# A decoder of six layers on one core: experts' weights prepared inside the experts' loop, and a rewritten quantised feed-forward

## The reference

```python
x = x + L0_attn(layernorm(x))     # 16 heads of 64, output projection, + x, layer norm, gamma, beta
x = x + L0_xattn(layernorm(x))    # attention over ctx (8, 64, 256), weights rounded to 256 levels
x = x + L0_ffn(layernorm(x))      # 8 groups: 256 -> 1024 -> 256, own weights for each group
x = x + L1_attn(layernorm(x))     # 8 experts, 2 for each row
x = x + L1_xattn(layernorm(x))    # masked attention over ctx, 16 heads of 16
x = x + L1_ffn(layernorm(x))      # quantised pair
```

## Time and profile before

| | us |
|---|---|
| median of 3 runs (2390.36 to 2404.99) | 2395.47 |
| the profiled execution | 2393.87 |
| its span, first to last instruction | 2392.2 |
| PE, DVE, ACT, POOL busy | 1696.3, 1606.5, 1374.0, 817.9 |
| PE's mean granted clock (1.00 is 2.4 GHz) | 0.855 |

### The profile page before, as it was taken

How to read it: one execution, slowest core, us unless ns; L and a number is a source line. 1 busy time by engine, 2 the same in 40 slices (tenths; PEclk the granted TensorE clock), 3 DMA queues, 4 the chain that set the end, 5 groups by cost and what they waited for, 6 DMA issues and landing times. The chain is left out here.

```text
span 2392.2 us, 43530 instructions
## 1 busy us (share of the span) xinstructions
PE 1696.3 (71%) x13405; PEld 1078.5 (45%) x13405; DVE 1606.5 (67%) x3129; ACT 1374.0 (57%) x2171; POOL 817.9 (34%) x751
## 2 busy tenths in 40 slices
PE   4889898989899898985899802223454677774855
PEld 1455555555555555553677601211222355553323
DVE  6867777787878778775233386735773767675774
ACT  3788888888878798881454412433553323333543
POOL 0434545454445454451000050570001444451042
PEclk9999999999999999996798955556666888987778
DMA  6222222222222222222122111422112111111002
GB/s 179 61 50 61 60 53 63 61 50 63 61 50 63 57 60 56 61 48 96 36 71 72 36 75 53 151 78 88 53 35 71 38 33 23 30 26 47 0 1 71
DMA packets 173941, 139.90 MB, mean 58 GB/s; under 512 B 83808, under 2 KB 155539, under 8 KB 173506
## 3 DMA queue, kind: packets, MB, share of 16 engines
q1 hardware_dynamic: 166850, 122.91, 19.8%
q0 software_dynamic: 6912, 14.71, 2.8%
HBM read 62.05 MB, written 20.97 MB: 35 GB/s over the span
## 5 line engine op out<-in xcount | busy, mean ns | idle before, releaser
L588 ACT ACTIVATE a_p_hi<-ps,a_probs_up,a_s_scale 128x512 f16<-128x512 f32 x512 | 397.9, 777 | 79.8 <-ACTq L586 79.2
L589 ACT ACTIVATE a_probs<-ps,a_probs_up,a_s_scale 128x512 f32<-128x512 f32 x512 | 398.4, 778 | 0.0
L690 DVE TENSOR_REDUCE a_top<-ps 128x2 f32<-128x1024 f32 x256 | 312.7, 1221 | 121.5 <-DVEq L689 121.5
L914 POOL TENSOR_TENSOR a_p_lo<-a_probs,a_p_hi 128x1024 f16<-128x1024 f32 x128 | 284.8, 2225 | 179.3 <-POOLq L913 163.9
L902 POOL TENSOR_TENSOR a_ops<-a_ident_down,a_top 64x256 f16<-64x256 f32 x256 | 158.8, 620 | 395.9 <-POOLq L897 387.4
L699 DVE TENSOR_TENSOR a_p_lo<-a_probs,a_p_hi 128x1024 f16<-128x1024 f32 x128 | 184.6, 1443 | 37.2 <-DVEq L698 37.2
L452 PE MATMUL ps<-a_ops 128*128 128x512 f16 x512 | 196.3, 383 | 13.5 <-PEq L450 13.5
L471 PE MATMUL ps<-a_v_hi,a_p_hi 128*128 128x65 f16 x2048 | 203.2, 196 | 2.2 <-PEq L466 2.2
L438 PE MATMUL ps<-a_qk,a_qd 128*128 128x512 f16 x512 | 153.4, 381 | 72.2 <-PEq L436 72.2
L474 PE MATMUL ps<-a_v_lo,a_p_hi 128*128 128x64 f16 x2048 | 203.2, 194 | 0.0
L475 PE MATMUL ps<-a_v_hi,a_p_lo 128*128 128x65 f16 x2048 | 203.0, 195 | 0.0
(11 more groups left out here) (482 smaller groups left out, 3782.2 us busy)
## 6 DMA issues: line engine op xcount, KB each, us to landing
a_ops<-a_qk SPq DMA_DIRECT2D x384, 128.0 KB, 2.4
f_w<-in_L_ffn_W_dram SPq DMA_DIRECT2D x16, 1024.0 KB, 7.4
a_qd<-a_qk SPq DMA_DIRECT2D x128, 64.0 KB, 2.3
g_a<-in_L_attn_gp_w_dram SPq DMA_DIRECT2D x8, 1024.0 KB
X<-in_x_dram SPq DMA_DIRECT2D x8, 512.0 KB, 9.9
expert_in<-g_w SPq DMA_DIRECT2D x8, 512.0 KB
g_a<-in_L_attn_dp_w_dram SPq DMA_DIRECT2D x8, 512.0 KB
e_x_in<-expert_in SPq DMA_DIRECT2D x8, 512.0 KB, 4.3
```

The source lines that it names most:

```text
L588: nc.scalar.activation(p_hi[:, h % 2, k, :], scores, ACT.Exp, bias=probs_up[:], scale=s_scale[:])
L589: nc.scalar.activation(probs[:, h % 2, k, :], scores, ACT.Exp, bias=probs_up[:], scale=s_scale[:]).then_inc(st_taken, 1)
L690: nc.vector.tensor_reduce(top[:, c % 2, 2 * pair:2 * pair + 2], ps[:, ROW:ROW + 2, :], AX.X, ALU.max).then_inc(row_taken, 1)
L914: nc.gpsimd.tensor_tensor(p_lo[:, h % 2, 2:KT, :], probs[:, h % 2, 2:KT, :], p_hi[:, h % 2, 2:KT, :], ALU.subtract).then_inc(p_made_pool, 1)
```

## The change

- **Self-attention.** DVE computes only minus the mean (128x1); ACT subtracts it (`centre`, 128x256, in heads 4, 6, 8, 10, ahead of `heads_out`); POOL multiplies by gamma (`times_gamma`, 128x512, in heads 8 and 12). DVE waits for both (`z_made`) in head 13. The last batch, behind the loop, is unchanged.
- **Middle.** `f_rows` and `f_rows_out` move behind the next scores and the last two groups of `w2T`, on PE and on ACT, and in the table of banks.
- **Experts.** `ExpertWeights` (below) has buffers of its own for two experts' raw weights; `upT` and `downT` hold three experts. Routing prepares experts 0 and 1 and sums the magnitudes of expert 2. In the loop, now written out for all eight experts, expert e's DVE queue rounds expert e+2, PE and ACT turn and copy expert e+1 in three pieces, all through PSUM bank 2, and ACT sums the magnitudes of e+3. The three Newton steps of an expert go from DVE to POOL. SP loads an expert's weights four ahead.
- **Masked attention** loads the pair's weights behind its mask.
- **Quantised pair.** The weights' peaks come before the row moments. The last tile of each sequence is normalised by ACT. The turns of rows and weights are interleaved. b2 is a column (two transposes of small rows), so its work is on 128x2 and not 128x256, and stands behind the semaphores that start the second pass. In the second pass outputs are computed with columns of the result as partitions (L2946's place: 512 columns each), scaled and shifted by ACT (first half) and DVE (second half), turned back by PE (eight f32 transposes a sequence) and added to `X` by DVE. PE takes a quarter of an output half behind each `h` bank. POOL has nothing left to do. The store of a sequence is issued when its rows are done, and `store_block` is gone.

The core of the diff:

```diff
# self_attention, DVE, head loop
-                            centre(t)
+                            nc.vector.tensor_scalar(less_mean[:, t:t + 1], ln_y.mean_var[:, t, 0:1], -1.0, None, ALU.mult)
+                            dve.drain().then_inc(y_means, 1)
# self_attention, ACT and POOL
+                    nc.scalar.activation(z[:, t, :], y[:, t, :], ACT.Identity, bias=less_mean[:, t:t + 1])
...
+                    nc.gpsimd.tensor_tensor(z[:, halves[half], :], z[:, halves[half], :], each(gam), ALU.mult)
# middle, PE (ACT likewise)
-                    if b:
-                        for c in range(DC):
-                            f_rows(b - 1, c)
                     if b + 1 < B:
                         scores(b + 1, bank_of["scores", b + 1])
                     if b < B:
                         turn_w2(b, 2)
                         turn_w2(b, 3)
+                    if b:
+                        for c in range(DC):
+                            f_rows(b - 1, c)
# experts: the new class
+class ExpertWeights:
...
+    def magnitudes(self, act, n):
+        nc, j = self.core.nc, n % 2
+        act.wait_ge(self.loaded[j], 32)
+        act.sem_inc(self.loaded[j], -32)
+        for i, part in self.parts:
+            nc.scalar.activation(self.junk[:, part], self.stage[:, j, part], ACT.Abs, accum_out=self.sums[:, j, i:i + 1])
+        act.drain().then_inc(self.part, 1)
+
+    def total(self, pe, n, bank):
+        nc, j = self.core.nc, n % 2
+        pe.wait_ge(self.part, 1)
+        pe.sem_inc(self.part, -1)
+        pe.wait_ge(self.out, 1)
+        nc.tensor.matmul(self.core.ps[:, bank, 0:2], self.ones[:], self.sums[:, j, :], start=True, stop=True).then_inc(self.total_full, 1)
+
+    def lower(self, dve, n, bank):
+        nc, j = self.core.nc, n % 2
+        dve.wait_ge(self.total_full, 1)
...
+        for i, part in self.parts:
+            nc.vector.tensor_scalar(self.below[:, part], self.stage[:, j, part], self.minus_half[:, j, i:i + 1], None, ALU.is_lt)
+
+    def ternary(self, dve, n):
...
+            nc.vector.scalar_tensor_tensor(out=self.w3[:, part], in0=self.stage[:, j, part], scalar=self.half[:, j, i:i + 1],
+                                           in1=self.below[:, part], op0=ALU.is_gt, op1=ALU.subtract)
+        dve.drain().then_inc(self.round, 1)
+        if n + 2 < self.E:
+            dve.drain().then_inc(self.used, 1)
+
+    def turn(self, pe, n, piece, bank):
...
+        pe.wait_ge(self.out, 1)
+        pe.sem_inc(self.out, -1)
...
+    def turned_out(self, act, n, piece, bank):
...
+        nc.scalar.activation(dst, self.core.ps[:, bank, :].bitcast(BF16), ACT.Copy).then_inc(self.out, 1)
# experts' loop, ACT
+                        weights_out(e + 1, 0)
+                        gate(j, 2)
+                        square_hidden(j, 2)
+                        weights_out(e + 1, 1)
+                        gate(j, 3)
+                        square_hidden(j, 3)
                         act.drain().then_inc(h_squared_all, 1)
                         if not first:
                             results((j + 1) % 2)
+                        weights_out(e + 1, 2)
                         if not last:
                             rows_out()
...
+                        if e + 3 < E:
+                            weights.magnitudes(act, e + 3)
# experts' loop, PE
+                        turn_weights(e + 1, 0)
                         up(e, 2)
+                        turn_weights(e + 1, 1)
                         up(e, 3)
                         if not first:
                             down(e - 1)
+                        turn_weights(e + 1, 2)
+                        if e + 2 < E:
+                            weights.total(pe, e + 2, WEIGHT_BANK)
# experts' loop, DVE
                         hidden(j, 2)
                         hidden(j, 3)
+                        if e + 2 < E:
+                            weights.lower(dve, e + 2, WEIGHT_BANK)
                         hidden_rows(e, j)
# hidden_rows, DVE: seed here, three Newton steps of four operations on POOL
-                        rsqrt(nc, dve, rstd[:], value[:], half[:], tmp[:])
...
+                        dve.drain().then_inc(seeded, 1)
+                        if e + 2 < E:
+                            weights.ternary(dve, e + 2)
+                        dve.wait_ge(rooted, 1)
# quantised_pair, PE, second pass
+                for b in range(B + 1):
                     for c in range(FC):
+                        if b < B:
+                            hidden_again(b, c)
+                        if b >= 2 and c == BACK_AT:
+                            turn_back(b - 2)
+                        if b:
+                            outputs(b - 1, c)
+                turn_back(B - 1)
```

More of the change, by code:

```diff
@@ L622, in batch @@
                             powers(h, k)
+                        if finish and h - 2 in PROJ_B:
+                            centre(PROJ_B[h - 2])
                         if h in TURN and (h > 1 or finish):
@@ L1906, in _ @@
[L1906 to L1917 removed]
+                    pe.sem_inc(weights.out, 1)
@@ L1919, in _ @@
+                    pe.sem_inc(weights.w3_used, 1)
+                    for n in range(2):
+                        weights.total(pe, n, WEIGHT_BANK)
+                        for piece in range(DC + 1):
+                            weights.turn(pe, n, piece, WEIGHT_BANK)
                 @block.vector
@@ L2241, in _ @@
                     gate(0, 1)
-                    expert(0, last=False, first=True)
-                    with act.Fori(0, E // 2 - 2) as pair:
-                        expert(1, last=False)
-                        expert(0, last=False)
-                    expert(1, last=False)
-                    expert(0, last=False)
-                    expert(1, last=True)
+                    for e in range(E):
+                        expert(e)
                     whole(r2[:], h[:, 1], h_round, r2_made)
@@ L2313, in _ @@
                     up(0, 1)
-                    expert(0, last=False, first=True)
-                    with pe.Fori(0, E - 2) as e:
-                        expert(e + 1, last=False)
-                    expert(E - 1, last=True)
+                    for e in range(E):
+                        expert(e)
                     turn_hidden()
@@ new lines, in hidden, with hidden_again @@
+                def hidden(b, c, bank):
+                    for m in range(DC):
+                        last = nc.tensor.matmul(ps[:, bank, :], w1T[:, m, c * P:(c + 1) * P], x8[:, m, b * S:(b + 1) * S],
+                                                start=(m == 0), stop=(m == DC - 1))
+                    return last
+                def hidden_again(b, c):
+                    pe.wait_ge(z_used, 1)
+                    pe.sem_inc(z_used, -1)
+                    hidden(b, c, c % 4).then_inc(h_full, 1)
@@ L2910, in _ @@
[L2910 to L2921 removed]
+                pe.wait_ge(w_out, 2)
@@ L2922, in _ @@
+                pe.sem_inc(w_out, -2)
+                for b in range(B):
                     pe.wait_ge(x8_made, 1)
@@ L3066, in _ @@
                 dve.sem_inc(a_taken, FC)
-                with dve.Fori(0, B) as b:
+                for b in range(B):
                     for c in range(FC):
```

771 lines of the change are left out of this document (420 added, 351 removed).

## The result

The changed kernel takes 2411.53 us against 2395.47 (medians of 17 runs each); the ratio is 1.0066, 95% interval 1.0052 to 1.008. That is 16 us slower, clear of the noise, where 2395 was forecast: inside the range of 2350 to 2420, but not "no change". The profiled execution has a span of 2408.6 us against 2392.2.

| stage | before | after | difference | forecast |
|---|---|---|---|---|
| load and self-attention | 1112.4 | 1099.3 | −13.1 | −16 |
| middle | 268.3 | 275.4 | **+7.1** | 0 |
| experts, routing | 239.5 | 228.8 | −10.7 | −13 |
| experts, loop | 212.9 | 282.8 | +69.9 | +71 |
| masked attention | 348.6 | 351.1 | +2.5 | +1 |

The account below looks back on a forecast made before the run. Chain of waits said nothing; engines' windows named PE in self-attention, POOL's DMAs in routing, DVE in the experts' loop. −16 + 0 − 13 + 71 + 1 − 42 = +1 on 2393.87: 2395 us, range 2350 to 2420.

Parts of the forecast that it names:

- the middle stage's term of 0: Middle stage: moved scores and w2T groups fill PE's waits, but ACT's copies come later; 0, bounds −15 and +7.
- The loop, +71: Experts' loop: DVE's added rounding, a wait for PE's total and delayed Newton cost 71 us; bounds +19 and +97.
- the new wait: Experts' loop: `lower(e+2)` waits for PE's total behind ACT's third weights copy; +7.2 us in experts 1 to 5.
- the held-up Newton: Experts' loop: POOL's Newton steps are held up by DVE's L2107 (`ternary`); +5.2 us in experts 1 to 5.
- Rival A: Experts' loop: Newton runs freely on POOL, so the loop costs +54; 2378 us, chance 0.20.
- Rival C: Experts' loop: PE's and ACT's turning on its path delays gates 2 and 3 by 3.9; 2421 us, chance 0.17.
- Routing, −13: Routing: six of eight experts' roundings leave, so POOL's indirect DMAs are less delayed; −13 us, bounds −17 to −10.
- rival D: Routing: no gain, its slow DMAs wait for something else than DVE's rounding; 2408 us, chance 0.08.
- Self-attention, −16: Self-attention: four `centre` calls leave DVE's queue, 2.3 us a batch in seven batches; −16 us, bounds −36 and +6.
- Rival B: Self-attention and loop: attention reaches its floor of −36 and Newton runs freely; 2358 us, chance 0.20.
- Masked attention, +1: Masked attention: two MB more behind its loads on SP cost 1 us, bounds 0 to +7.
- The pair, −42: Quantised pair: earlier start, no POOL adds, shorter second-pass sequences and store; −42 us, bounds −50 and −25.

Follow-up runs that it names:

- The last two kernels: Changed kernel with experts of before, f_rows behind the scores only and later pair outputs: 2341.14 us; then also turning back and DVE's adds later: 2325.01 us.

## Why the prediction was wrong, point by point

- **Where it failed: the middle stage's term of 0.** The text saw the two more `w2T` copies ahead of `f_xnT`, priced them as 0.7 us late, and set that against waits won in slow-clock batches. The waits by themselves were nearly that: 3.05 − 2.06 = 1.0 us a batch, where 0.7 was costed. Two things failed. The 1.5 us won in slow-clock batches needs turns at the low clock, and only the first batch had them (1.92 us for its eight, 1.04 to 1.06 in the others, which ran at full clock); that batch had no wait at its outputs, and in five of the other seven PE waited 2.96 to 3.05 us. And the gap was priced by its length alone: over the outputs behind each of these five waits the granted clock was 0.58 to 0.68, and they took 5.37 to 6.32 us, 1.7 to 2.6 more than at full clock. Four batches then had a period of 26.9 to 27.6 us; the same four of before took 24.06 in two, at full clock, and 26.1 and 28.5 in the others. The upper bound of +7 was met, and is too low if the old order is worth 262.
- **The rest of the miss: four terms 1.5 to 3 us short.** In attention, routing and the pair a step was priced too well (below); for masked attention the cause is open. Each shortfall is also within what a stage moves between traces, so their sizes are not shown one by one. A sum of +1 out of terms of −42 to +71 hung on all of them.
- **The loop, +71: right, 69.9.** An expert of 1 to 5 took 11.4 to 11.9 us more, where 12.4 was costed; the 3 us taken off for the branches no run shows by itself, so part of the agreement is luck. Both disputed steps were shown apart: the new wait (moving `lower` gave 20.2, moving the copy 8.1) and the held-up Newton (back on DVE 12.0). Its first operation was not the long one, as forecast, but the second and third, 2.14 and 1.06: the first slipped in before `ternary` began. Rival A, Newton running freely, fell with that. Rival C was to decide at 3 us between hidden 2 and hidden 3, and there were 3.3; but that mark was badly set, since the forecast's own 2.4 + 0.95 lies above it. The delay was the 0.9 that was costed, not 3.9, the granted clock over the loop was 0.61 and not 0.50, and C fell.
- **The rule on ports.** POOL's operations waited for L1764, which reads two operands in SBUF, and in the kernel with `lower` late also for L1756 (one operand in SBUF, f32 to bf16; 1.22 us for an operation of 0.20). The Trainium skill, "SBUF — State Buffer", section "Who interferes with whom", gives the first as the second input on the shared read port and lists `tensor_scalar` among those that can take both port pairs in a 2-port mode; by that rule the traces agree in both cases. One operation was not held: in the kernel with `lower` late POOL's L2379 began 0.04 us behind L1764 and took 0.20.
- **Routing, −13: 10.7.** The mean fell to 1064 ns, not to 1030, since the two roundings that stayed cost 5.8 us and not a quarter of 17; rival D fell.
- **Self-attention, −16: 13.1.** Three of the four heads fell by 0.6 to 1.0 (8.67, 8.62 and 8.82 to 7.86, 8.05 and 7.82), the eighth by 0.05, which I had at 0.6. Two other heads grew: the seventh by 0.3, which goes away with ACT's subtraction, and the twelfth from 6.61 to 7.29. What of this last belongs to the change is open: leaving GpSimd's multiply out did not take it back. Rival B, the floor of −36, fell: with ACT's share gone too it was −21.
- **Masked attention, +1: 2.5 in this pair of executions.** Over the ten kernels here with the load the stage took 350.8 to 360.1, over the four without 348.6 to 356.0. Whether the load costs 0 or 5 us is not settled.
- **The pair, −42: 39.2.** Start 11.5 (9.8 forecast), the step between the passes 3.5 (3.2), first sequence 12.7 (14.2), store 10.1 (9.9); the later sequences gained 1.4 and not 5.2, because the eighth rounding of a sequence stood one bank ahead of the outputs that need it. The last two kernels show it and win it back: a sequence falls from 9.3 to 8.0 us with outputs and turns both later.
- **Slips in the working.** The waits at the turns were 14.8 us in all, not 16. 64 times 1.27 is 81.3, not 81.8. And 53.3 us over 234 matmuls is 0.228 each, which makes 7.3 us a sequence and not 7.05: up to 2 us of the pair's −42. None of them changes which rival was right.

## What to carry to other kernels

When work is moved into an engine's wait, follow its result: here the queue that copies the result out (ACT) set how far it could move, and one step less far turned +7 us into −12 in the stage (−10 in the kernel). A wait that an engine takes in the middle of its queue is paid by all that stands behind it, so a step with a late input belongs behind the step that starts another engine: `lower` behind the seed cost nothing and hid Newton. And when a wait is removed and the time doesn't change, look for the next wait of the same length before giving the idea up; it was one constant away.

## What the runs showed of the hardware

- Eight f32 matmuls of 512 columns, over the fourteen traces: behind a wait of 2.96 to 3.14 us they took 5.37 to 6.33 us in all 39 cases, with a granted clock of 0.58 to 0.68 over them. Without a wait they took 3.67 to 3.70 in 23 of 34 cases, behind one of 1.06 to 1.74 us in 16 of 39. So the low clock comes without a wait of 3 us too, but behind such a wait it never stayed away, and 1.7 us or more were paid beyond the wait itself.
- GpSimd operations of 128x4 (0.20 us) took 2.14 and 1.06 us beside a DVE operation with two operands in SBUF: each ended 0.06 to 0.08 us behind the end of one of DVE's two parts (1706.81 and 1708.01). So GpSimd got one operation done for each part.
- Code that had not changed took 262 to 269 us (middle), 205 to 210.6 (pair) and 349 to 356 (masked attention without the load) in different traces, each with its own granted clock. A difference of 5 us in a stage needs more than one trace.
